# Projection of a decoder layer: sums of squares and the rounding of weights on ScalarE, remainders on VectorE, and GpSimd left with one multiplication into a single buffer

## The reference, cut to what matters

```python
q = jnp.einsum('bsd,ed->bse', x, Wq).reshape(bsz, seqlen, HQ, D)    # HQ = 32 heads, D = 128
k = jnp.einsum('bsd,ed->bse', x, Wk).reshape(bsz, seqlen, HK, D)    # HK = 8
v = jnp.einsum('bsd,ed->bse', x, Wv).reshape(bsz, seqlen, HK, D)
q = _rmsnorm(q, q_norm_w)       # t * rsqrt(mean(t*t) + 1e-6) * w, over each head's 128 columns
k = _rmsnorm(k, k_norm_w)
q = _rope(q, pos)               # concat(t1*cos - t2*sin, t2*cos + t1*sin), t1 and t2 the halves
k = _rope(k, pos)
...
o = jnp.einsum('bhqk,bkhd->bqhd', probs, v_all)
return jnp.einsum('bse,de->bsd', o, Wo)
```

## Time and profile before

| | |
|---|---|
| median of 3 runs | 2378.04 us |
| the profiled execution | 2378.56 us |
| its span in the trace | 2376.7 us |
| TensorE busy in the span | 2321.4 us (98%) |
| VectorE | 1520.9 us (64%) |
| ScalarE | 1336.1 us (56%) |
| GpSimd | 808.0 us (34%) |
| mean granted TensorE clock | 0.991 of full speed |

### The profile page before, as it was taken

One profiled execution on the slowest core, in us unless ns is written; L12 is line 12 of the kernel. 1 busy time (PEld: TensorE's weight loads), 2 busy tenths in 40 slices (PEclk: granted clock), 3 DMA queues, 4 the chain that ended last, 5 costly groups with the idle time before them and its releaser, 6 DMA issues.

```text
span 2376.7 us, 47878 instructions
## 1 busy us (share of the span) xinstructions
PE 2321.4 (98%) x14320; PEld 2008.1 (84%) x14320; DVE 1520.9 (64%) x3994; ACT 1336.1 (56%) x3820; POOL 808.0 (34%) x858
## 2 busy tenths in 40 slices
PE   8999999989999999999999999999999999999998
PEld 7777777777989888889999999999998788888886
DVE  5999999993656666666666666666665443344333
ACT  4777777773656666666666666666666222222222
POOL 5788878882223333332222222222223110111011
PEclk9999999999999999999999999999999999999999
DMA  5344444437988888888888998999886233333331
GB/s 205 89 125 103 107 106 123 106 87 265 357 278 289 282 289 283 288 287 287 289 290 288 292 295 291 289 291 292 290 288 230 91 104 93 103 101 104 93 104 47
DMA packets 400352, 488.57 MB, mean 206 GB/s; under 512 B 63136, under 2 KB 334752, under 8 KB 397216
## 3 DMA queue, kind: packets, MB, share of 16 engines
q1 hardware_dynamic: 363296, 351.93, 48.1%
q0 software_dynamic: 36864, 134.23, 17.0%
HBM read 397.89 MB, written 88.08 MB: 204 GB/s over the span
## 4 chain that ended last, share of the span: by engine, by line
PE 73%; DVE 17%; issue 7%; SPq 1%; DMA 1%; ACT 0%; POOL 0%; DVEq 0%; ACTq 0%; POOLq 0%
PE s_bank L1020 19%; PE o_bank L1032 17%; PE pt L1067 9%; PE proj L1519 5%; PE proj L1521 5%; PE proj L1520 4%; DVE q_t L689 4%; DVE wo_early L697 4%; DVE part_s L675 3%; PE o_bank L1048 2%; DVE k_t L702 2%; PE acc L747 1%; PE acc L748 1%; PE acc L749 1%; DVE probs L987 1%
## 5 line engine op out<-in xcount | busy, mean ns | idle before, releaser
L987 DVE CUSTOM_DVE_ANT_0 probs<-s_bank,mask 128x544 f32<-128x544 f32 x512 | 371.0, 725 | 429.2 <-PE s_bank L1020 426.9
L941 ACT ACTIVATE probs<-probs,neg_max 128x544 f32<-128x544 f32 x512 | 383.9, 750 | 408.2 <-DVE neg_max L987 408.2
L1020 PE MATMUL s_bank<-k_t,q_t 128*128 128x288 f32 (+1 forms) x2048 | 557.6, 395 | 7.0 <-DVE neg_max L987 2.5
L1032 PEld LDWEIGHTS o_bank<-p_t,v_c 128*128 128x128 f32 x4096 | 528.0, 192 | 29.3
L1032 PE MATMUL o_bank<-p_t,v_c 128*128 128x128 f32 x4096 | 540.6, 275 | 0.0
L1020 PEld LDWEIGHTS s_bank<-k_t,q_t 128*128 128x128 f32 x2048 | 349.7, 191 | 67.7 <-DVE neg_max L987 11.6
L138 POOL DMA_INDIRECT v_c<-in_v_rows,v_row x256 | 255.3, 997 | 301.5 <-PE o_bank L1032 261.0
L507 POOL TENSOR_TENSOR q_t<-normed,v_c 128x256 f32<-128x256 f32 x320 | 303.9, 970 | 95.3 <-ACT normed L564 66.8
L747 PE MATMUL acc<-w_hi,x_hi 128*128 128x512 f32 x764 | 306.3, 401 | 27.7 <-POOL w_lo L469 27.7
L1067 PE MATMUL pt<-ident,probs 128*128 128x128 f32 x2048 | 311.2, 275 | 0.0
L748 PE MATMUL acc<-w_lo,x_hi 128*128 128x512 f32 x764 | 303.6, 397 | 0.0
(11 more groups left out here) (154 smaller groups left out, 3293.3 us busy)
## 6 DMA issues: line engine op xcount, KB each, us to landing
k_t<-in_k_pages SPq DMA_DIRECT2D x1024, 128.0 KB
q_spill<-wo_early SPq DMA_DIRECT2D x512, 64.0 KB, 1.8
q_t<-q_spill SPq DMA_DIRECT2D x64, 512.0 KB
o_spill<-o_t SPq DMA_DIRECT2D x64, 512.0 KB, 5.0
raw<-o_spill SPq DMA_DIRECT2D x64, 512.0 KB, 3.5
k_t<-in_w_qkv SPq DMA_DIRECT2D x11, 1024.0 KB, 5.7
v_spill<-wo_early SPq DMA_DIRECT2D x8, 1024.0 KB, 7.0
k_spill<-wo_early SPq DMA_DIRECT2D x128, 64.0 KB, 1.8
```

What stands on the lines that cost most here:

```text
L941: nc.scalar.activation(probs[:, j % SLOTS_P], probs[:, j % SLOTS_P], ACT.Exp, scale=-1.0, bias=neg_max[:, j % 2:j % 2 + 1], accum_out=row_ ...
L987: nc.vector.tensor_tensor_reduce(out=probs[:, j % SLOTS_P], in0=s_run, in1=mask[:, par], scale=-SCALE, scalar=3.0e38, op0=ALU.add, op1=ALU ...
L1020: last = pe.matmul(s_bank[:, columns].rearrange("p (s t) -> p s t", t=PSIZE), q_t[:, par, g], k_t[:, par, slots, g], start=True, stop=True)
L1032: last = pe.matmul(o_of(n), v_c[:, par, c, g * HD:(g + 1) * HD], p_t[:, i, c], start=g < QUAD and c == 0, stop=False)
```

## The change

- ScalarE sums the squares of all four heads itself (four instructions with a running sum), so that VectorE's `total` and its semaphore go.
- ScalarE rounds the weights (`round_weights`), one chunk each where t is 1, 4, 7 or 10. VectorE makes the remainder (`remainder`) one tile later. GpSimd's `split` goes for slices 2 to 11. The first slices are split as before (`split_second` is the old code with slice 1 written in).
- `part_c` has one buffer in place of two, and cross(n) waits for `roped_done`, m in place of m - 1: for the addition of the tile just before it.
- The steps of a tile lie further apart. ScalarE runs square(n), root(n-1), drain(n-2). VectorE runs go_straight(n-3), add(n-4), invert(n-1), turn(n-4) and, on some tiles, a remainder.

```diff
-    OWN_SUMS = 2
...
-        part_c = part(q_t[:, 0].rearrange("p g n -> p (g n)"), 0, [P, 2, HS, HD])
+        part_c = part(q_t[:, 0].rearrange("p g n -> p (g n)"), 0, [P, HS, HD])
...
+        ROUND_AT = (1, 4, 7, 10)
...
-            def split(s, c):
-
-                par = s % 2
+            def split_second(c):
+
                 if c == 0:
-                    w_landed(pool, s)
-                    at_least(pool, mm_done, NT * (s - 1))
-                nc.gpsimd.tensor_copy(w_hi[:, par, c], w_raw[:, par, c]).then_inc(w_hi_done, 1)
-                pool.wait_ge(w_hi_done, DC * s + c + 1)
-                nc.gpsimd.tensor_sub(w_lo[:, par, c], w_raw[:, par, c], w_hi[:, par, c].bitcast(F32))\
-                    .then_inc(w_split, 1)
+                    w_landed(pool, 1)
+                nc.gpsimd.tensor_copy(w_hi[:, 1, c], w_raw[:, 1, c]).then_inc(w_hi_done, 1)
+                pool.wait_ge(w_hi_done, DC + c + 1)
+                nc.gpsimd.tensor_sub(w_lo[:, 1, c], w_raw[:, 1, c], w_hi[:, 1, c].bitcast(F32)).then_inc(w_split, 1)
...
                 pool.wait_ge(drained, m + 1)
-                at_least(pool, roped_done, m - 1)
+                at_least(pool, roped_done, m)
                 cr = crossed[kind(n)]
                 for lo, hi in ((0, HALF), (HALF, 0)):
                     last = nc.gpsimd.tensor_mul(
-                        part_c[:, i, :, lo:lo + HALF], normed[:, i, :, hi:hi + HALF],
+                        part_c[:, :, lo:lo + HALF], normed[:, i, :, hi:hi + HALF],
...
-            for n in range(NT, TILES + 2):
-                s, t = n // NT + 1, n % NT
-                if is_qk(n - 1):
-                    cross(n - 1)
-                if t in (3, 6, 9, 12) and s < NSL:
-                    split(s, t // 3 - 1)
+            for n in range(NT, NT + QKS):
+                cross(n)
...
+            def round_weights(s, c):
+                w_landed(act, s)
+                act.wait_ge(mm_done, NT * (s - 1))
+                nc.scalar.activation(w_hi[:, s % 2, c], w_raw[:, s % 2, c], ACT.Copy).then_inc(w_hi_done, 1)
+
             def root(n):
                 m, i = qk_before(n), n % 2
-                act.wait_ge(summed, m + 1)
+                act.wait_ge(squared, m + 1)
+                at_least(act, rstd_done, m - 1)
...
                 act.wait_ge(mm_done, n + 1)
-                for h in range(OWN_SUMS):
-                    nc.scalar.activation(squares[:, i, h], acc_of(n)[:, h * HD:(h + 1) * HD], ACT.Square,
-                                         accum_out=sumsq[:, i, h:h + 1])
-                nc.scalar.activation(squares[:, i, OWN_SUMS:HS],
-                                     acc_of(n)[:, OWN_SUMS * HD:SLICE].rearrange("p (h d) -> p h d", d=HD),
-                                     ACT.Square).then_inc(squared, 1)
+                at_least(act, rooted, qk_before(n) - 1)
+                for h in range(HS):
+                    last = nc.scalar.activation(squares[:, i, h], acc_of(n)[:, h * HD:(h + 1) * HD], ACT.Square,
+                                                accum_out=sumsq[:, i, h:h + 1])
+                last.then_inc(squared, 1)
...
                 if is_qk(n - 1):
-                    drain(n - 1)
-                if is_qk(n):
-                    root(n)
-                else:
+                    root(n - 1)
+                if is_qk(n - 2):
+                    drain(n - 2)
+                if kind(n) == "v":
                     stage_values(n)
+                s, t = n // NT + 1, n % NT
+                if t in ROUND_AT and 1 < s < NSL:
+                    round_weights(s, ROUND_AT.index(t))
...
+            def remainder(s, c):
+                dve.wait_ge(w_hi_done, DC * s + c + 1)
+                nc.vector.tensor_tensor(w_lo[:, s % 2, c], w_raw[:, s % 2, c], w_hi[:, s % 2, c].bitcast(F32), ALU.subtract)\
+                    .then_inc(w_split, 1)
...
-            def total(n):
-                dve.wait_ge(squared, qk_before(n) + 1)
-                nc.vector.tensor_reduce(sumsq[:, n % 2, OWN_SUMS:HS], squares[:, n % 2, OWN_SUMS:HS], AX.X, ALU.add).then_inc(summed, 1)
-
-            for n in range(NT, TILES + 3):
-                if is_qk(n):
-                    total(n)
+            for n in range(NT, TILES):
+                if is_qk(n - 3):
+                    go_straight(n - 3)
+                if is_qk(n - 4):
+                    add(n - 4)
                 if is_qk(n - 1):
-                    go_straight(n - 1)
-                if is_qk(n):
-                    invert(n)
-                if is_qk(n - 3):
-                    turn(n - 3)
-                if is_qk(n - 2):
-                    add(n - 2)
+                    invert(n - 1)
+                if is_qk(n - 4):
+                    turn(n - 4)
+                s, t = n // NT + 1, n % NT
+                if t - 1 in ROUND_AT and 1 < s < NSL:
+                    remainder(s, ROUND_AT.index(t - 1))
```

More of the change, by code:

```diff
@@ L329, in project @@
         squared = sem("squared")
-        summed = sem("summed")
         rooted = sem("rooted")
@@ L488, in _ @@
             for c in range(DC):
-                split(1, c)
+                split_second(c)
             pool.wait_ge(minus_done, 2)
@@ L681, in invert @@
                 dve.wait_ge(rooted, m + 1)
+                at_least(dve, drained, m - 1)
                 nc.vector.reciprocal(rstd[:, i], rms[:, i]).then_inc(rstd_done, 1)
@@ L688, in add @@
                 at_least(dve, staged_qk, m - 1)
-                nc.vector.tensor_tensor(roped[:, i], part_s[:, i], part_c[:, i], ALU.add)\
+                nc.vector.tensor_tensor(roped[:, i], part_s[:, i], part_c[:, :, :], ALU.add)\
                     .then_inc(roped_done, 1)
```

## The result

The changed kernel takes 2365.18 us (median of 6 runs, 2360.92 to 2369.84), against 2378.03 before. The ratio is 0.9942, 95% interval 0.993 to 0.9953: faster by 13 us, about half of what was forecast. The profiled execution took 2368.99 us, one of the two slowest of the six, with a span of 2367.1.

A forecast was written before the change was run, and what follows sets the result against it. VectorE and GpSimd taking turns at shared ports was taken as the bound. Afterwards a ring of 457.6 us from 65.9 ends the stage at 554.0: 2378.56 less 26.7 is 2351.9, forecast 2352, range 2333 to 2370.

The forecast's parts named there:

- turns at the shared port: Projection: VectorE's two-input instructions and GpSimd's take turns, 2.90 of 3.02 us a tile, and this bounds the kernel before.
- the reduction: VectorE's reduction, 0.41 us, takes no turn; its removal was given no gain.
- the ring: Single part_c buffer: addition and crossings wait for each other, 2.77 us a plain tile, 3.2 with a remainder.
- The start: Tile pipeline: VectorE's first multiplication comes later, at 65.9 us against 62.29 before.
- idle for over 0.3 us a tile: Sign against the forecast: VectorE's addition idle for over 0.3 us a tile.
- multiplications of about 1.2 us: Sign for the forecast: VectorE's multiplications take about 1.2 us on plain tiles, more on the others.
- TensorE as the bound: Rival, 21 in 100: projection tiles follow at TensorE's 2.745 us, time 2335.
- The handover: Projection to next stage: last load, the queries, issued at 546.0, still 8 us ahead of the end at 554.0.
- a first matmul that waits for a load: Sign against the forecast: the next stage's first matmul waits for a load.
- From there on the two kernels are the same: After the projection: same distance to the end as before, so the 26.7 us gain stays.
- slower: Rival, 8 in 100: the addition's wait for GpSimd makes the ring cost more; at a 0.53 us handoff, 2403.
- no change: Rival, 6 in 100: handoff of about 0.3 us, or ScalarE at 3.0 us a tile, time 2378.

The follow-up runs named there:

- e9: Kernel before with only the sums moved: ScalarE sums the squares of all four heads, VectorE's reduction goes; 2349.28 us, 0.9881.
- e3: Changed kernel with part_c in two buffers again and the crossing let go one addition earlier; 2338.86 us, 0.9832.
- e5: Changed kernel (one buffer) without the 40 remainders of slices 2 to 11, ScalarE still rounding; 2335.8 us, 0.9818.
- e1: Changed kernel with the second store of values issued before the first two batches' loads, not between them; 2363.49 us, 0.9945.
- e11: Changed kernel (one buffer) with second batch's gathers held until the projection ends and second value store between first batch's page loads; 2362.97 us, 0.9939.
- e4: Kernel before with only the split moved: ScalarE rounds the weights, VectorE makes the remainders; 2349.25 us, 0.9879.
- e8: Changed kernel with two buffers, second batch's gathers held back, second value store between first batch's page loads; 2334.86 us, 0.9815.
- e7: Changed kernel with two buffers and the second batch's gathers held until TensorE is through the projection; 2339.33 us, 0.9839.
- e13: e8 with the output weights' six loads spread over batches 2 to 7 and their splitting begun at batch 10; 2333.84 us, 0.9805.

## Why the prediction was half right

**The bound before.** I wrote that turns at the shared port, 2.90 of 3.02 us, are the bound. That step failed. Turns are only part of it: the bound was VectorE's queue, its own 0.33 + 0.57 + 0.09 + 0.60 + 0.57 = 2.16 us a tile plus its waits for turns. In e9 no turn is gone, and tiles are 2.83 us apart, less than the 2.90 of the turns' sum. Taking away a reduction that takes no turn gained 28 us (e9), as much as moving the split (e4). The earlier trace rows had hinted at it: VectorE busy for 48.31 of 48.31 us. I gave the reduction nothing; alone it is worth as much as the split. In the whole change this error cost little, since the ring took over as the bound. That was luck: the forecast of the end needed only the ring, not the account of what had bound the kernel before.

**The ring.** The mechanism was right and was sized well: 2.77 forecast, 2.82 measured on plain tiles (the addition after an idle moment takes 0.69, not 0.64; handoffs 0.15 and 0.09, against 0.14 and 0.10), 3.2 and 3.20 on those with a remainder, where the turns went as told: remainder between the crossings, multiplication behind them. The start was 66.37 against 65.9, and 159 steps took 462.4 us against 457.6. So the stage ended at 559.2, not 554.0: 5.2 us. The forecast for the profiled run was 2351.9, it took 2368.99, and the 17.1 us between them are these 5.2, the 6.0 of the wait and the 5.9 behind it. The median, 2365.18, misses the 2352 by 13. That the single buffer is the price was told; with two buffers the same edits gain 39 us (e3). The 3.20 was booked only for the 40 tiles. e5 shows that the remainders also hold the plain tiles at 2.82 where the ring can do 2.74.

Two of the signs that I listed don't fit my own sum. I called myself wrong if the addition was idle for over 0.3 us a tile; it is idle for 0.69 on plain tiles, and a multiplication that ends between the two crossings leaves about that much. I also expected multiplications of about 1.2 us there. They take 0.76: the multiplication comes up 0.53 us behind the first crossing's start (304.60 against 304.07), so that it waits some 0.2 us, not 0.5 or more. Only tiles with a remainder have 1.23.

**TensorE as the bound.** This rival is what happens with two buffers or without remainders: in both, ScalarE waits for TensorE (39.3 and 38.4 us from 100 to 480 us). Its price, 2335, is that of e5 (2335.8) and near e3 (2338.9). In the change itself it didn't come true.

**The handover.** Here the sum failed. I wrote that the last load was issued "still 8 us ahead", and took the issue for the arrival. In the profiled run the queries' load was issued at 551.92, 7.3 us ahead of 559.2, as forecast. But the value store issued at 552.39 released ScalarE only at 563.93, and in e1 the queries took from 556.94 to 564.71. I also looked at one load and not at the store that stands in the same queue, though it gates ScalarE's last four tiles. It cost 6.0 us, and 4.1 more at the low clock. e1 shows that the store was not alone: with it out of the way, the queries arrived at nearly the same time (5.12 us of wait). The sign that I had given for this, a first matmul that waits for a load, came in another form: it waited for ScalarE, and ScalarE for a store.

**"From there on the two kernels are the same"** failed as well, by the other 1.8 us of 5.9. The changed kernel waits for queries for 4.2 us in the batches behind (at 625.17 and 648.09), the kernel before for 2.0 (at 657.06). What is won at the stage's end can be lost behind it: removed at the first batch, the wait came back at the third (e11), where SyncE issued its loads late. Full DMA engines alone don't explain that, with a share of 0.44 just before those loads, and no run isolates the cause. The handover edits moved the median by 4 us on two buffers and by 2 on the changed kernel, and neither is clear of the noise, while a shorter pipeline keeps most of its gain.

**ScalarE** did not bound, as said, with 39.63 of 46.61 us. The waits for `w_lo` went, as said. The rivals "slower" and "no change" rested above all on the handoff from GpSimd; it is 0.09 us.

## What to carry to other kernels

An engine that is busy for all of a period is the first suspect for the bound, whatever it spends the time on: its own short instructions count as much as the waits inside the long ones. But waits inside instructions stretch, so that such an engine can also be keeping another's pace (VectorE in e3). Who waits for whom decides. Count a single buffer between two engines as a ring of both durations and two handoffs, and let an occasional extra instruction in it be judged by the phase that it forces on the others, not only by its length. Where a stage ends earlier, follow each load and store in the queue to its arrival, and look at what the issuing engine waits for and at the busy share of the DMA engines behind it.

## What was not expected of the hardware

A wait of TensorE ahead of the first batch's scores, 5.96 us (after), 5.12 (e1) or 2.88 (e4), is followed by some 12 us with a granted clock of 0.54 to 0.60, with units (from one group of four score matmuls to the next) of 3.0 us in place of 2.0. TensorE came to the same work at full clock where it hadn't waited (before, e3, e8, e11). But a wait isn't needed: in e7 and e13 it also began at full clock, and from 542.5 to 547.7 us had 0.67, with no wait over 0.94 us ahead of it. What tells these two from e8 stays open. And one pair of crossings takes 1.44 us where no VectorE instruction comes between them, and 1.89 where a multiplication or a remainder does.
